# Graph kernel: ends of steps turned by TensorE, one stored reset mask, and a new order for the last two batches of the first edge layer

## The reference

```
h = (x @ W.T).reshape(N, H, F)                       # 8 heads of 32
alpha = leaky(sum(h[src]*a_src) + sum(h[dst]*a_dst)) # per edge and head
exp_a = exp(alpha - segment_max(alpha, dst)[dst])
agg   = segment_sum(h[src] * exp_a / segment_sum(exp_a, dst)[dst], dst)
```

## Time and profile before

| what | value |
|---|---|
| median of 3 runs | 1919.19 us (1916.95 to 1919.61) |
| the profiled execution | 1912.22 us |
| its span | 1910.5 us |
| POOL busy in the span, share | 1012.8 us, 53% |
| DVE busy in the span, share | 1426.3 us, 75% |
| TensorE busy in the span, share | 1321.5 us, 69% |
| mean granted clock of TensorE | 0.844 |

### The profile page before, as it was taken

One profiled execution on the slowest core, in us unless ns is written; L12 is line 12 of the kernel. 1 busy time (PEld: TensorE's weight loads), 2 busy tenths in 40 slices (PEclk: granted clock), 3 DMA queues, 4 the chain that ended last, 5 costly groups with the idle time before them and its releaser, 6 DMA issues. The chain is left out here.

```text
span 1910.5 us, 29161 instructions
## 1 busy us (share of the span) xinstructions
PE 1321.5 (69%) x7038; PEld 919.6 (48%) x7038; DVE 1426.3 (75%) x3659; ACT 925.1 (48%) x3196; POOL 1012.8 (53%) x1082
## 2 busy tenths in 40 slices
PE   5436655665665569998867778777878778563286
PEld 4324433443443457776544555555555554452164
DVE  5458888888988953436868899999999997776043
ACT  2444556555555343322440677777777773231033
POOL 2377777777776000000517777777777775101555
PEclk9767887787777759999986899999999999775599
DMA  5766767667666119000358888888888884325564
GB/s 121 202 175 203 207 200 215 206 207 217 210 208 186 56 30 356 3 1 6 138 199 260 268 265 251 265 261 265 269 261 269 263 266 139 110 69 109 187 192 137
DMA packets 174910, 356.04 MB, mean 186 GB/s; under 512 B 29303, under 2 KB 70825, under 8 KB 174621
## 3 DMA queue, kind: packets, MB, share of 16 engines
q0 software_dynamic: 58192, 175.85, 30.6%
q1 hardware_dynamic: 116558, 178.33, 29.8%
HBM read 268.46 MB, written 89.75 MB: 187 GB/s over the span
## 5 line engine op out<-in xcount | busy, mean ns | idle before, releaser
L796 POOL DMA_INDIRECT e_rows<-h_rows,src_col x416 | 412.9, 993 | 127.0 <-issue 123.6
L1282 POOL DMA_INDIRECT e_rows<-kv_rows,src_col x320 | 306.5, 958 | 99.9 <-issue 66.8
L1042 PE MATMUL e_sum<-e_rows,e_of_dst 128*128 128x264 f32 x832 | 291.1, 489 | 98.3 <-DVE e_rows L887 81.8
L1501 ACT ACTIVATE e_rows<-e_rows 128x64 f32<-128x64 f32 x1152 | 281.4, 335 | 0.3
L1564 PE MATMUL e_query<-q,e_to_dst 128*128 x1248 | 203.5, 294 | 78.3 <-DVE e_rows L1335 58.1
L1042 PEld LDWEIGHTS e_sum<-e_rows,e_of_dst 128*128 128x128 f32 x832 | 172.5, 235 | 141.5 <-DVE e_rows L887 88.9
L1604 PE MATMUL e_sum<-e_rows,e_of_dst 128*128 128x260 f32 x640 | 185.2, 412 | 1.8 <-POOL e_rows L1212 1.2
L1564 PEld LDWEIGHTS e_query<-q,e_to_dst 128*128 128x128 bf16 x1248 | 120.3, 100 | 134.0 <-issue 94.8
L969 ACT ACTIVATE e_rows<-e_rows 128x32 f32<-128x32 f32 x832 | 181.0, 305 | 0.1
L1423 DVE TENSOR_TENSOR acc<-acc,e_sum 128x260 f32 x346 | 145.4, 420 | 41.5 <-DVE acc L1423 20.4
L1282 POOL DMA_INDIRECT x<-kv_rows,src_col x96 | 91.5, 953 | 72.9 <-POOLq L2087 38.5
(11 more groups left out here) (415 smaller groups left out, 2676.0 us busy)
## 6 DMA issues: line engine op xcount, KB each, us to landing
step_of<-e_of_dst SPq DMA_DIRECT2D x104, 256.0 KB, 2.3
e_of_dst<-step_of SPq DMA_DIRECT2D x104, 256.0 KB, 3.7
sorted_rows<-zeros SPq DMA_DIRECT2D x1, 14560.0 KB
rows<-sorted_rows SPq DMA_DIRECT2D x56, 260.0 KB, 2.9
e_rel<-step_rel SPq DMA_DIRECT2D x26, 512.0 KB, 4.3
step_to<-e_to_dst SPq DMA_DIRECT2D x26, 512.0 KB, 5.9
e_to_dst<-step_to SPq DMA_DIRECT2D x52, 256.0 KB, 4.4
e_rows<-h_rows,src_col POOLq DMA_INDIRECT x416, 3.3
```

The costliest lines, as they stand in the source:

```text
L796: pool.indirect_dma_start(out=g[t // BATCH % R][:, t % BATCH, :], out_offset=None, in_=k.h_rows[:, :], in_offset=bass.IndirectOffsetOnAxis ...
L1042: pe.matmul(psm[t % NB], of_dst[q][:, s % GROUP, :], g[m % R][:, s, :], start=True, stop=True).then_inc(summed, 1)
L1282: pool.indirect_dma_start(out=rows_at(t, 1)[:, 0, :], out_offset=None, in_=k.kv_rows[:, :], in_offset=bass.IndirectOffsetOnAxis(ap=k.src_c ...
L1501: ins = act.activation(x, x, ACT.Copy, scale=row[:, plo + h:plo + h + 1])
```

## The change

Five edits, all in the opening and in the edge layers:

1. The ends and windows of steps no longer go through HBM. `ends_f` is written eight columns wide, and TensorE multiplies it, and the windows `win_f`, by the identity: 12 matmuls in fp32 (`rows_over_steps`), ahead of the turn of window 20, into PSUM banks that are free by then. DVE copies two of the results out of PSUM (`ends_r`, `win_row`) and computes `joined` from the third and the copy. 12 stores and 2 loads by DMA go, and with them SP's wait between them.
2. The reset mask is stored once (`step_cut`, one DMA of 104x4x132 floats in place of eight DMAs that wrote 416x12x132). Where it is loaded, the source is read eight times (first layer) or four times (second) over.
3. The four memsets at the start of `edges_first` move from POOL to DVE.
4. Batches 24 and 25 of `edges_first` are written out in another order, given below.
5. In those two batches POOL makes the messages of the second and third group (16 instructions) after its last gather, in place of DVE (8 instructions of 2 steps each); TensorE's sums wait for them.

```diff
+                c.inc(v.tensor_copy(ends_f[:, 0, :, :], rows_f[:, :, 0, 0].unsqueeze(2).to_broadcast(eight)))
+                c.inc(v.tensor_copy(ends_f[:, 1, :, :], rows_f[:, :, 0, P - 1].unsqueeze(2).to_broadcast(eight)))
...
             def joins_of_steps():
-                v.wait_ge(reread, 32)
                 c.link(v.memset(k.joined[:, :, :], 1.0))
+                v.wait_ge(pe_done, 4)
+                first, last = ps_a[0:8, 0:STEPS], ps_b[0:8, 0:STEPS]
+                c.inc(v.tensor_copy(ends_r[:, :], last))
+                c.inc(v.tensor_copy(k.win_row[:, 0:STEPS], wins))
...
+            def rows_over_steps():
+                pe.wait_ge(k.dve_steps, marks["columns"])
+                for sc in range(SC):
+                    at, one = slice(sc * SP, (sc + 1) * SP), k.ident[0:SP, 0:SP]
+                    pe.matmul(ps_a[0:8, at], ends_f[:, 0, sc, :], one, start=True, stop=True)
+                    pe.matmul(ps_b[0:8, at], ends_f[:, 1, sc, :], one, start=True, stop=True)
+                    mm = pe.matmul(wins[:, at], win_f[:, sc:sc + 1], one, start=True, stop=True)
+                mm.then_inc(pe_done, 1)
...
+                if w == 4 * UNR:
+                    rows_over_steps()
...
-            store_cuts(H0, k.step_cut8)
+            sp.dma_start(k.step_cut[:, :].rearrange("(c p) e -> p c e", p=SP), cut[:, :, :]).then_inc(stored, 16)
             store_rows(2)
-            store_cuts(H1, k.step_cut4)
...
+            steps = k.step_cut[m * BATCH:(m + 1) * BATCH, :]
+            sp.dma_start(cut[m % R][:, :],
+                         steps.unsqueeze(1).to_broadcast([BATCH, H, P + 4])).then_inc(steps_in[m % R], 16)
...
+        for m, q in BY_POOL:
+            pool.wait_ge(prob_in_rows, m + 1)
+            for s in range(q * GROUP, (q + 1) * GROUP):
+                row = g[m % R][:, s, :]
+                vals = row[:, 0:D].rearrange("p (h f) -> p h f", h=H)
+                ins = pool.tensor_tensor(vals, vals, row[:, D:D + H].unsqueeze(2).to_broadcast([P, H, F]), ALU.mult)
+            ins.then_inc(msg_by_pool, 1)
...
-        for m in range(LAST_BATCH):
+        for m in range(LAST_BATCH - 1):
...
+        m = LAST_BATCH - 1
+        w = load_windows(m)
+        hot(m, 0)
+        rescale(m, w)
+        values(m, 0, 0)
+        values(m, 0, 1)
+        scores(LAST_BATCH)
+        hot_alone(m, 1)
+        hot_alone(m, 2)
+        step_maxima(LAST_BATCH)
+        add(m, range(0, 2), w)
+        across_steps(LAST_BATCH)
+        add(m, [2], w)
+        hot_alone(m, 3)
+        add(m, [3], w)
+        factors(LAST_BATCH)
+        last_w = load_windows(LAST_BATCH)
+        add(m, range(4, 8), w)
+        differences(LAST_BATCH, w, [8, 9, 10])
+        hot(LAST_BATCH, 0)
+        hot(LAST_BATCH, 1)
+        add(m, range(11, BATCH), w)
+        values(LAST_BATCH, 0, 0)
+        values(LAST_BATCH, 0, 1, groups=2)
+        rescale(LAST_BATCH, last_w)
+        hot_alone(LAST_BATCH, 2)
+        hot_alone(LAST_BATCH, 3)
+        add(LAST_BATCH, range(BATCH), last_w)
```

More of the change, by code:

```diff
@@ L372, in rows_of_steps @@
                 c.link(v.tensor_copy(rows_f[:, :, :, :], rows[:, :, :, :]))
-                c.inc(v.tensor_copy(ends_f[:, 0, :], rows_f[:, :, 0, 0]))
-                c.inc(v.tensor_copy(ends_f[:, 1, :], rows_f[:, :, 0, P - 1]))
-                marks["ends"] = c.count
+                eight = [SP, SC, 8]
+                c.inc(v.tensor_copy(ends_f[:, 0, :, :], rows_f[:, :, 0, 0].unsqueeze(2).to_broadcast(eight)))
+                c.inc(v.tensor_copy(ends_f[:, 1, :, :], rows_f[:, :, 0, P - 1].unsqueeze(2).to_broadcast(eight)))
                 for j in range(SC):
@@ L391, in columns_of_steps @@
                 c.inc(v.tensor_copy(k.src_col[:, :], ps_b[:, 0:STEPS]))
+                marks["columns"] = c.count
             def joins_of_steps():
-                v.wait_ge(reread, 32)
                 c.link(v.memset(k.joined[:, :, :], 1.0))
-                c.link(v.tensor_tensor(k.joined[:, 0, 1:STEPS], ends_r[:, 0, 1:STEPS], ends_r[:, 1, 0:STEPS - 1],
+                v.wait_ge(pe_done, 4)
+                first, last = ps_a[0:8, 0:STEPS], ps_b[0:8, 0:STEPS]
+                c.inc(v.tensor_copy(ends_r[:, :], last))
+                c.inc(v.tensor_copy(k.win_row[:, 0:STEPS], wins))
+                c.wait()
+                c.link(v.tensor_tensor(k.joined[:, 0, 1:STEPS], first[:, 1:STEPS], ends_r[:, 0:STEPS - 1],
                                        ALU.not_equal))
-                c.link(v.tensor_tensor(single[:, :], ends_r[:, 0, :], ends_r[:, 1, :], ALU.not_equal))
+                c.link(v.tensor_tensor(single[:, :], first, ends_r[:, :], ALU.not_equal))
                 c.inc(v.tensor_tensor(k.joined[:, 1, 0:STEPS], k.joined[:, 0, 0:STEPS], single[:, :], ALU.max))
@@ L788, in _ @@
     def _(pool):
-        pool.memset(run[:, 0:1], NEG).then_inc(filled, 1)
-        pool.memset(back[:, :], NEG).then_inc(filled, 1)
-        pool.memset(ctxt[:, :, :], NEG).then_inc(filled, 1)
-        pool.memset(fac[:, :], 0.0).then_inc(filled, 1)
         for t in range(STEPS):
@@ L888, in values @@
             if half:
-                ins.then_inc(hot_ready, 1)
+                ins.then_inc(hot_ready, groups)
         def add(m, steps, w):
@@ L905, in _ @@
         load_windows = windows(v, "dve_w")
-        v.wait_ge(filled, FILLED)
+        c.inc(v.memset(run[:, 0:1], NEG))
+        c.inc(v.memset(back[:, :], NEG))
+        c.inc(v.memset(ctxt[:, :, :], NEG))
+        c.inc(v.memset(fac[:, :], 0.0))
         for acc in accs:
@@ L939, in _ @@
                 add_bias(m // 4 - 1)
-        w = load_windows(LAST_BATCH)
-        rescale(LAST_BATCH, w)
-        for q in range(GROUPS):
-            hot(LAST_BATCH, q)
-            if q not in BY_ACT:
-                values(LAST_BATCH, q, 0)
-                values(LAST_BATCH, q, 1)
-            if q:
-                add(LAST_BATCH, range((q - 1) * GROUP, q * GROUP), w)
-        add(LAST_BATCH, range(BATCH - GROUP, BATCH), w)
+        m = LAST_BATCH - 1
[11 more added lines that the diff above has]
+        add(m, [2], w)
+        hot_alone(m, 3)
+        add(m, [3], w)
[12 more added lines that the diff above has]
+        add(LAST_BATCH, range(BATCH), last_w)
     @block.scalar
```

57 lines of the change are left out of this document (17 added, 40 removed).

## The result

| | before | after |
|---|---|---|
| median | 1919.40 us (1916.95 to 1924.81, 6 runs) | 1906.42 us (1900.50 to 1909.37, 6 runs) |
| profiled execution, span | 1912.22, 1910.5 | 1900.50, 1898.8 |
| mean granted clock | 0.844 | 0.846 |

The ratio is 0.9924, with a 95% interval of 0.9905 to 0.9943: faster by 13 us, where 15.2 was forecast. The sum of two terms hides how they differ: up to the first gather the opening gave what was expected, the last two batches gave half of it.

What follows compares the result with a forecast made beforehand. Bound: ACT's wait for h_rows in the opening, then POOL's 416 gathers, then DVE and TensorE behind the last gather. Opening -9.2 and tail -6.0 give -15.2: 1897.0 profiled, 1904.0 us with 7.0 carried over; range 1898.5 to 1911.0.

Steps and rivals of the forecast that it cites:

- Column stores and wait: Opening: without the column stores ACT's wait for h_rows goes, minus 8.9 us; TensorE's 12 added matmuls cost plus 1.3.
- Mask and memsets: End of the opening: mask stored once, minus 1.2 us (0 to 1.9); memsets moved to DVE, minus 0.4 (0 to 0.7).
- Opening: Everything up to POOL's first gather: minus 9.2 us, bounds -6.0 and -11, first gather at 67.3.
- Tail: Last two batches of the first edge layer, reordered and with POOL's messages: minus 6.0 us, bounds -2.1 to -7.8.
- Differences 4.2 earlier at best; with TensorE at 0.50 on the way I take 4.0: Behind the last gather: DVE ends batch 25's differences 4.0 us earlier, at 631.1 instead of 635.1.
- its third rival: Last two batches: POOL and DVE hold each other up, each of six instructions waiting one message (0.58); total -12.4, chance 0.10.
- The steps behind: Batch 25 after its differences: first sum 4.4 us later, 16 sums in 9.8, then the last add, at 645.9.
- My forecast's own warning: Last two batches: matrices of 1.2 us beside POOL's messages were listed among the signs that the forecast is wrong.
- TensorE did not hold the tail: First rival: batch 25's sums run at half clock to the end; tail -2.1, total -11.3, 1907.9 us, chance 0.12.
- The gathers kept their pace: Fourth rival, edge layer: mask loads and moved HBM tensors double the gathers' loss, +19.5 against -15.2, 1923.5 us, chance 0.07.
- The second rival: Opening gives less: early h_rows stores delay POOL's edge-row gathers by 2 us, longer joins show; total -12, 1907, chance 0.11.
- the range that the bounds made: Whole kernel: the bounds of opening and tail give -8.1 to -18.8 us, 1900.4 to 1911.1.

Runs made afterwards that it cites:

- the moved column stores: Kernel before with its 12 column stores (ends and windows of steps) moved behind the first four stores of h_rows: 1929.52 us, ratio 1.0037.
- the copies back in the new opening: Kernel after with the reset mask stored twelve times over in seven DMAs and read from the copies: 2127.72 us, ratio 0.9954, on a slower chip.
- row and factors in PSUM: Kernel after, matrices and rescaling of batches 24 and 25 reading number row and factors from PSUM: 2137.32 us (1.0013, slower chip); 1901.84 us (0.9929, third chip).

## Why the prediction was right, and where it was not

*Column stores and wait: right.* ACT's last copy came 7.2 us earlier (70.46 to 63.27); -8.9 + 1.3 = -7.6 was forecast. The wait and the slow clock behind it gave the 8.9 to the digit: window 10's copy came at 44.68 for 44.65, and the seven windows behind it took 8.46 (44.68 to 53.14). The matmuls took 56.41 - 54.17 = 2.2 for the 2.0 forecast, so with the 0.5 of TensorE's wait that they filled they cost 1.7 of the 8.9, where 1.3 was forecast. That the wait must not stand ahead of any store of h_rows, the moved column stores showed.

*Mask and memsets: 1.6 forecast, 2.2 seen* (ACT's last copy to first gather, 6.0 before and 3.8 after). The wait of SP that was to fall by 1.2 fell from 3.8 to 1.8, and with the copies back in the new opening it was 4.5. By that run the mask is worth 2.6, outside the 0 to 1.9 that it was given. But it is one profile, and the 2.6 is more than the 2.2 for both edits together. The same distance was 6.0 in the kernel before, 7.2 in the run of the last two batches alone (69.62 to 76.78) and 5.0 in that of the moved columns (82.98 to 88.02), all three with the mask stored twelve times over. That the term was too small is likely; its size is open.

*Opening: first gather 67.05 for 67.3.* The clock held in that execution. In others it did not (below), and the first gather then comes at 68.7 to 70.2. The term -9.2 is therefore the good end of what this opening gives where before takes 1916 to 1920, -6.3 to -9.6. Of the 9.4 at the first gather, 0.9 was lost along the gathers, for which the forecast had nothing.

*Tail: 3.3 of 6.0.* The step that failed is "Differences 4.2 earlier at best; with TensorE at 0.50 on the way I take 4.0". They came no earlier at all: 20.27 behind the last gather for 20.29. Of the missing 4.0, the first matrix took 2.7 (3.37 for 0.68) and the first rescaling 0.4 (0.57 for 0.16). The forecast priced this at 0.36 for each of two or three of DVE's instructions, 0.4 in all, and in batch 24 at 0.7 in its third rival. Most of the other 0.9 is a wait of DVE for TensorE's sums, 0.71 ahead of 622.04 and 0.27 ahead of 623.86, with TensorE at 0.50 from 616 to 620; the forecast had 0.2 for that. The steps behind were right: from the differences to the first sum 4.2 (forecast 4.4), the sums 9.05 (forecast 9.8), the last add 0.6 behind. With the two SBUF inputs gone, at the price of the row's copy, differences come 17.4 and the last add 31.2 behind. That this meets the forecast's 31.0 is partly luck: the first sum is still 1.0 late (21.6 for 20.6), and the sums are 0.75 faster than forecast.

*The rivals.* The third one happened, POOL and DVE holding each other up, but in batch 24, for which it had 0.7, and much less in batch 25: the four rescaling instructions there took 2.49 for some 1.17, and TensorE's sums hid it, since they ran their 9.05 without a wait for an emptied bank. It was priced at one message for each instruction; one matrix was held from the third message to the end of the seventh. My forecast's own warning ("matrices of 1.2 us beside POOL's messages") came true threefold. The Trainium skill ("SBUF — State Buffer", "Who interferes with whom") names the condition: a DVE instruction with two SBUF inputs contends with a GpSimd instruction that reads SBUF, one with at most one SBUF input does not, outside of the modes in which DVE uses both ports. The runs with row and factors in PSUM agree (0.69 and 0.16 beside messages). Read as one message's wait, 0.58, its rule that the second waits for the whole of the first would have been too cheap: the traces show 2.7 in three executions and 0.3 in a fourth, and the measurement decides. TensorE did not hold the tail: its last sums ran at 1.00. The gathers kept their pace but for 0.9 us in all, 995 ns. The second rival, an opening that gives less, is half true: not by late edge rows, but by the clock, and in five profiles of seven.

*The total* was 1906.4 for 1904.0. The profiled pair has 8.5 at the last gather and 3.3 behind it, 11.8 of the 15.2, and 1258.2 and 1258.3 us behind the layer. The medians differ by 13.0, because the kernel before was profiled 7.2 under its median and the kernel after 5.9: 1.3 of the agreement is luck. The largest error, 2.7 in the tail, lies inside the range that the bounds made. The two halves run alone (-11.9 and -4.7) add up to 16.6 where both together gave 13.0; with intervals of 0.2% on each that is no contradiction. In the layer, where the marks are firm, they nearly do add up: 8.5 and 2.7 alone, 8.5 and 3.3 together.

## What to carry to other kernels

Before work is handed from VectorE to GpSimd, list the VectorE instructions that will run beside it and count their SBUF inputs, and price a contended one against a whole row of back-to-back messages, not one; taking one operand of each from PSUM freed 2.8 us here for a copy of 0.29. A DMA queue that waits for small stores holds up whatever stands behind the wait: moving the wait down the list made it cost more here, and removing the stores is what helped.

## What the runs showed of the hardware that was not expected

- *A DVE instruction can be held through several GpSimd instructions in a row.* The matrix was held 2.7 us beside back-to-back messages of 0.58 each in three executions (3.37, 3.36 and 3.35 us long), and 0.3 us in the one where it started 1.89 rather than 1.23 us behind the first of them. GpSimd pays too: its eight messages took 5.07 beside the long matrix, where the longest took 1.05 in place of 0.61, 5.59 where the two took turns, 4.62 with no contention. What decides who goes first was not settled.
- *Behind a longer gap of TensorE ahead of window 10 the opening is 1.7 to 3.3 us longer.* TensorE waits there for xn. In the kernel after's first profile, then its second, with the clock of two stretches behind it:

```profile
42.15 0.44 PE L554 MATMUL ps_t<-ident,xn 128*128 128x128 f32 x2 [2.64 <-DVE xn L213]
```

```profile
42.41 0.69 PE L554 MATMUL ps_t<-ident,xn 128*128 128x128 f32 x2 [4.36 <-DVE xn L213]
```

```profile
44.00:46.00 2.00, 2.00 (x7) 0.50 0.00 0
46.00:48.00 2.00, 2.00 (x7) 0.50 0.72 197
```

xn comes at nearly the same time (42.15 and 42.41), but in the second TensorE had finished the work before it earlier and idled longer; its clock was granted 0.50 behind the gap, the last copy came at 66.34 in place of 63.27, and the first gather at 70.14. Of the seven profiles of this opening from chips where before takes 1916 to 1920, five show the fall, behind waits of 3.07 to 4.36 us, and two don't, behind 2.41 and 2.64; their first gathers come at 68.7 to 70.2 and at 66.9 to 67.05. This compares executions; the gap was not varied on purpose, and filling it was not tried.
- *4-byte columns land late with idle DMA engines.* Twelve stores of 104 elements kept SP waiting 8.3 us behind the last issue, while the engines' share was 0.05 and less, and 0.00 for the last 7 of them (53 to 60 us). In the kernel before it was 49.13 - 40.43 = 8.7, with four stores of h_rows between:

```profile
38.80 1.63 SPq L627 DMA_DIRECT2D step_win<-win_i  x4
...
49.13 0.29 SPq L632 DMA_DIRECT2D ends_r<-step_ends  x1
```

What the time goes into is open.
